# Selective-scan kernel: the carry between chunks added to column 0 of the scans' inputs, B rows and bias operands moved from ScalarE to TensorE, split of one product at 312 columns

## What is computed

```
layer 0:  v = group_norm(x, 32 groups);  u, z = split(v @ in_proj)          192 channels each
          u = silu(causal_conv_4(u) + conv_b)
          dt, B, C = split(u @ x_proj)                                      6 + 16 + 16
          delta = softplus(dt @ dt_proj + dt_bias);  A = -exp(A_log)
          h[t] = exp(delta[t] * A) * h[t-1] + delta[t] * B[t] * u[t]        192 channels x 16 states, 4096 steps
          y[t] = sum over states of h[t] * C[t]  + D * u[t]
          x = x + layer_norm((y * silu(z)) @ out_proj) * gamma + beta
layer 1:  t = t + linear attention(layer_norm(t));  t = t + feed-forward(layer_norm(t))   fp8 products, fp16 sums
```

## Time and profile before

| what | value |
|---|---|
| median of three runs | 2514.06 us |
| each run | 2515.68, 2513.10, 2514.06 us |
| span of the profiled execution, first to last instruction | 2508.8 us |
| what the median has beyond that span | 5.3 us |
| instructions in the profile | 35019 |
| mean granted TensorE clock | 0.987 |
| HBM read, written | 400.33 MB, 91.88 MB |

### The profile page before, as it was taken

One profiled execution on the slowest core, in us unless ns is written; L12 is line 12 of the kernel. 1 busy time (PEld: TensorE's weight loads), 2 busy tenths in 40 slices (PEclk: granted clock), 3 DMA queues, 4 the chain that ended last, 5 costly groups with the idle time before them and its releaser, 6 DMA issues.

```text
span 2508.8 us, 35019 instructions
## 1 busy us (share of the span) xinstructions
PE 2142.1 (85%) x10314; PEld 826.0 (33%) x10314; DVE 2454.5 (98%) x2391; ACT 2314.7 (92%) x3960; POOL 2414.8 (96%) x655
## 2 busy tenths in 40 slices
PE   6788888888888888888888888888888888888878
PEld 3334434323323323323333323323323333333323
DVE  7999999999999999999999999999999999999986
ACT  5777777999999999999999999999999999999977
POOL 4999999999999999999999999999999999999991
PEclk8999999999999999999999999999999999999979
DMA  6555555556656656566566566566566565566542
GB/s 243 189 185 172 195 185 184 202 198 207 209 202 205 207 201 212 201 205 206 204 206 214 194 208 212 195 210 208 198 210 211 197 207 201 192 206 203 186 142 75
DMA packets 171388, 494.54 MB, mean 197 GB/s; under 512 B 23072, under 2 KB 44704, under 8 KB 154240
## 3 DMA queue, kind: packets, MB, share of 16 engines
q1 hardware_dynamic: 171200, 492.30, 57.9%
HBM read 400.33 MB, written 91.88 MB: 196 GB/s over the span
## 4 chain that ended last, share of the span: by engine, by line
POOL 40%; issue 40%; DVE 15%; PE 3%; ACT 1%; DMA 0%; POOLq 0%; DVEq 0%; SPq 0%; ACTq 0%
POOL R L676 20%; DVE R L1277 11%; POOL D L649 9%; POOL R L672 7%; POOL du L642 3%; DVE D L1261 2%; POOL D L658 2%; PE G L1568 1%; PE Y L1568 0%; DVE q L1357 0%; DVE dl L1287 0%; DVE G L1302 0%; DVE h L1471 0%; DVE h L1478 0%; PE Y L1645 0%
## 5 line engine op out<-in xcount | busy, mean ns | idle before, releaser
L1277 DVE TENSOR_TENSOR_SCAN R<-DA,R,D 128x512 f32<-128x512 f32 x1344 | 1630.2, 1263 | 1.0 <-ACT DA L840 1.0
L840 ACT ACTIVATE DA<-ds,kept_w 128x512 f32<-128x512 f32 x1536 | 1054.8, 688 | 139.9 <-DVE R L1277 127.1
L676 POOL TENSOR_TENSOR R<-R,Cs 128x2048 f32<-128x2048 f32 x255 | 970.9, 3819 | 4.0 <-DVE R L1277 2.6
L649 POOL TENSOR_TENSOR D<-us,Bs 128x2048 f32<-128x2048 f32 x193 | 736.9, 3818 | 8.8 <-DMA us<-lo_d 8.8
L672 POOL TENSOR_TENSOR R<-R,Cs 128x4096 f32<-128x4096 f32 x64 | 476.5, 7446 | 0.1
L1261 DVE TENSOR_TENSOR D<-us,PB 128x2048 f32<-128x2048 f32 x191 | 356.8, 1868 | 6.3 <-DMA us<-lo_d 6.3
L1645 PE MATMUL Y<-R,kept_w 128*32 128x512 f32 x2048 | 266.1, 615 | 13.9 <-POOL R L672 12.8
L1602 PE MATMUL G<-un,wcv 96*128 96x512 f32 x512 | 251.6, 614 | 29.5 <-ACT h L907 29.5
L1277 DVE TENSOR_TENSOR_SCAN R<-DA,D 128x512 f32<-128x512 f32 x192 | 221.7, 1204 | 2.1 <-ACT DA L840 2.1
L1605 PE MATMUL G<-un,wcv 96*64 96x256 f32 x1024 | 138.5, 392 | 60.1 <-ACT xq L888 58.9
L1568 PE MATMUL G<-st,kept_w 128*64 128x256 f32 (+1 forms) x384 | 108.9, 485 | 53.5 <-ACT st L802 53.5
(11 more groups left out here) (240 smaller groups left out, 3437.5 us busy)
## 6 DMA issues: line engine op xcount, KB each, us to landing
Bs<-bc_d SPq DMA_DIRECT2D x128, 512.0 KB, 5.6
us<-lo_d SPq DMA_DIRECT2D x64, 1024.0 KB, 6.3
ds<-lo_d SPq DMA_DIRECT2D x64, 1024.0 KB, 8.4
Cs<-bc_d SPq DMA_DIRECT2D x128, 512.0 KB, 4.7
us<-hi_d SPq DMA_DIRECT2D x64, 512.0 KB, 6.8
ds<-hi_d SPq DMA_DIRECT2D x64, 512.0 KB, 5.5
lo_d<-dl SPq DMA_DIRECT2D x64, 256.0 KB, 2.0
lo_d<-du SPq DMA_DIRECT2D x64, 256.0 KB, 2.0
```

Of the source, the lines that this page charges most:

```text
L649: nc.gpsimd.tensor_tensor(shaped(D[:, s % NDBU, :, :], s), low(us, s) if s in LOWS else high(us), of_states(Bs, s), ALU.mult).then_inc(don ...
L676: nc.gpsimd.tensor_tensor(shaped(R[:, s, :, 0:T], s), shaped(R[:, s, :, 1:S], s), of_states(Cs, s), ALU.mult).then_inc(hc_done.sem, 1)
L840: nc.scalar.activation(DA[j % NDA][:, :], ds[:, i, :], ACT.Exp, scale=A[:, j:j + 1]).then_inc(exp_done.sem, 1)
L1277: nc.vector.tensor_tensor_scan(R[:, s, q, 1:S], DA[j % NDA][:, :], D[:, s % NDBU, q, :], before, ALU.mult, ALU.add).then_inc(scanned.sem, 1)
```

## The change

Three things. First, in a continuing chunk the scans of quads 1 to 5 no longer take their start value from R. In its place exp(delta[0] * A) * R's last column is added to column 0 of D: `first_product` (delta[0] * A, VectorE), `first_decay` (exp, ScalarE), `carries` (times R's last column, VectorE) for quads 1 to 3 together and for quads 4 and 5 together, and `take_carry` (add to column 0, VectorE) for each quad. Quad 0 keeps the pointer operand. The new calls stand in VectorE's iteration here: first_product (g, 0) behind scan (0, 0); carries (g, 0) behind scan (0, 1); take_carry 1 behind gate part 1; take_carry 2 behind scan (1, 0); first_product (g, 1) behind scan (2, 2); take_carry 3 behind scan (2, 3); carries (g, 1) behind scan (3, 1); take_carry 4 behind scan (3, 3); take_carry 5 behind scan (4, 2). ScalarE runs first_decay (g, 0) behind decay (0, 2) and first_decay (g, 1) behind decay (3, 0).

Second, `put_b` moves from ScalarE to TensorE: a matmul of st's 32 rows of B and C with a selection matrix writes B's rows spread over 128 rows into PB, without waiting for Bs. It stands first in TensorE's iteration (quad 1), behind out_proj (g - 1) (quad 3) and behind variance (g - 1, 1) (quad 0 of g + 1). st becomes double-buffered, with B and C in rows 0 to 31, dt in rows 32 on and a constant row of ones, so its eviction is a plain copy. The bias of the convolution becomes a 97th row of its first tap's matmul, and the epsilon under three logarithms a 97th row of the averaging matmul (rows of ones in un, sq and fsq, set by four memsets at the start).

Third, SPLIT[3] goes from 232 to 312 columns.

```diff
-SPLIT = {3: 232}
+SPLIT = {3: 312}
...
+        def goes_on(k):
+
+            return 0 <= k <= LAST and k % CH > 0
...
-        wcv = sb("wcv", [C, TAPS, 2 * LOW])
+        wcv = sb("wcv", [C + 1, TAPS, 2 * LOW])
...
-        un = sb("un", [C, HALO + T])
+        un = sb("un", [C + 1, HALO + T])
...
-        st = sb("st", [128, T])
+        st = sb("st", [128, 2, T])
...
+        first = sb("first", [128, QUADS, QUAD])
...
+        first_arg, first_exp = Continued("first_arg", 2), Continued("first_exp", 2)
+        first_carry, first_in = Continued("first_carry", 2), Continued("first_in", 5)
...
+        def first_of(v):
+
+            return first[:, 1:QUAD, :] if v == 0 else first[:, QUAD:QUADS, :]
...
             sp_eng.dma_start(cwb, I["conv_w"].partition_broadcast(C)).then_inc(cwb_in, 16)
+            sp_eng.dma_start(wcv[C:C + 1, 0, :], I["conv_b"]).then_inc(cb_in, 16)
...
-                    nc.scalar.activation(u[:, place(k) % 2, part(v)], src[v], ACT.Silu, bias=cb[:, v:v + 1])\
+                    nc.scalar.activation(u[:, place(k) % 2, part(v)], src[v], ACT.Silu)\
...
             def state_rows(k, src):
                 act.wait_ge(back_mm.sem, back_mm.at(k, 1))
-                act.wait_ge(back_mm.sem, back_mm.at(k - 1))
-                if there(k - 1):
-                    act.wait_ge(bc_out, count(k - 1, 16, 16))
-                nc.scalar.activation(st[:, :], src[:, :], ACT.Identity, bias=one_row).then_inc(st_done.sem, 1)
+                act.wait_ge(b_put.sem, b_put.at(k - 2))
+                if there(k - 2):
+                    act.wait_ge(bc_out, count(k - 2, 16, 16))
+                nc.scalar.copy(st[0:64, k % 2, :], src[0:64, :]).then_inc(st_done.sem, 1)
...
-            def put_b(k, s):
-                if k == 0 and s == 1:
-                    return
-                h, w = LOWS[s]
-                if s == 3 and place(k + 3) == 0 and later(k + 3):
-                    act.wait_ge(gn_act.sem, gn_act.at(k + 3, 4))
-                act.wait_ge(b_in[h], count(k, 16, 16))
-                act.wait_ge(dbu_d.sem, dbu_d.at(k, BY_DVE[s] - steps_to(k, s)))
-                n = SPLIT.get(s, T)
-                nc.scalar.copy(PB[:, 0:n], Bs[:, h, w, 0:n]).then_inc(b_put.sem, steps_to(k, s))
...
+            def first_decay(k, v):
+                act.wait_ge(first_arg.sem, first_arg.at(k, 1 + v))
+                nc.scalar.activation(first_of(v), first_of(v), ACT.Exp).then_inc(first_exp.sem, 1)
...
-                nc.scalar.activation(rs[:, :], src[0:C, :], ACT.Ln, bias=epsn[0:C, :]).then_inc(post_ln.sem, 1)
+                nc.scalar.activation(rs[:, :], src[0:C, :], ACT.Ln).then_inc(post_ln.sem, 1)
...
+            step(nc.vector.memset(sq[C:C + 1, :], 1.0))
+            step(nc.vector.memset(fsq[C:C + 1, :], 1.0))
+            step(nc.vector.memset(un[C:C + 1, :], 1.0))
+            step(nc.vector.memset(st[64:65, :, :], 1.0))
             credit(nc.vector, by_dve)
...
                     dve.wait_ge(summed.sem, summed.at(k - 1, s + 1))
-                before = 0.0 if place(k) == 0 else R[:, s, q, T:S]
+                    if s and goes_on(k):
+                        dve.wait_ge(first_in.sem, first_in.at(k, s))
+                before = R[:, s, q, T:S] if s == 0 and goes_on(k) else 0.0
...
+            def first_product(k, v):
+                dve.wait_ge(d_in[v], count(k, 16, 16))
+                if v == 0:
+                    a = A[:, QUAD:4 * QUAD].rearrange("p (s q) -> p s q", q=QUAD)
+                    d = ds[:, 0:QUAD, 0].unsqueeze(1).to_broadcast([128, 3, QUAD])
+                    o = first_of(v)
+                else:
+                    a = A[:, 4 * QUAD:BLOCKS].rearrange("p (w i) -> p w i", i=2)
+                    d = ds[:, QUAD:QUADS, 0].unsqueeze(1).to_broadcast([128, 4, 2])
+                    o = first_of(v).rearrange("p s (w i) -> p (s w) i", i=2)
+                nc.vector.tensor_tensor(o, a, d, ALU.mult).then_inc(first_arg.sem, 1)
+
+            def carries(k, v):
+                dve.wait_ge(first_exp.sem, first_exp.at(k, 1 + v))
+                dve.wait_ge(scanned.sem, scanned.at(k - 1, (4, 6)[v] * QUAD))
+                quads = slice(1, QUAD) if v == 0 else slice(QUAD, QUADS)
+                nc.vector.tensor_tensor(first_of(v), first_of(v), R[:, quads, :, T], ALU.mult).then_inc(first_carry.sem, 1)
+
+            def take_carry(k, s):
+                dve.wait_ge(first_carry.sem, first_carry.at(k, 1 if s in LOWS else 2))
+                if s in BY_DVE:
+                    dve.wait_ge(dbu_d.sem, dbu_d.at(k, BY_DVE[s]))
+                else:
+                    dve.wait_ge(dbu_p.sem, dbu_p.at(k, BY_POOL[s]))
+                at = D[:, s % NDBU, :, 0]
+                nc.vector.tensor_tensor(at, at, first[:, s, :], ALU.add).then_inc(first_in.sem, 1)
...
-                        last = mm(o[:, :], wcv[:, t, 0:LOW], un[:, t:t + T], start=(t == 0), stop=(t == TAPS - 1))
+                        last = mm(o[:, :], wcv[0:rows_of(t), t, 0:LOW], un[0:rows_of(t), t:t + T], start=(t == 0), stop=(t == TAPS - 1))
...
+            def put_b(k, s):
+                if k == 0 and s == 1:
+                    return
+                if s == 3 and place(k + 3) == 0 and later(k + 3):
+                    pe.wait_ge(gn_act.sem, gn_act.at(k + 3, 4))
+                pe.wait_ge(st_done.sem, st_done.at(k))
+                pe.wait_ge(dbu_d.sem, dbu_d.at(k, BY_DVE[s] - steps_to(k, s)))
+                n = SPLIT.get(s, T)
+                one(PB[:, 0:n], bsel[:, BY_DVE[s] - 1, :], st[0:2 * STATE, k % 2, 0:n]).then_inc(b_put.sem, steps_to(k, s))
...
-        "wx": wx, "one_row": consts["one_row"], "dtw": dtw, "D": cols_of(np.asarray(L0_conv_D)[chan], 2),
+        "wx": wx, "dtw": dtw, "D": cols_of(np.asarray(L0_conv_D)[chan], 2),
+        "bsel": np.stack([np.arange(32)[:, None] == 8 * h + 2 * (row[None, :] % NSUB) + w
+                          for h, w in ((0, 0), (0, 1), (1, 1))], 1),
```

More of the change, by code:

```diff
@@ L142, in at @@
                 return count(k, 1, LEAD + 1 - FIRST * CH)
+        class Continued(Progress):
+            def at(self, k, n=None):
+                return (k - batch(k) - 1) * self.per + (self.per if n is None else n)
         rows_of_R = sb("R", [128, QUADS, QUAD, S + 3])
@@ L171, in build @@
         soon = cols["kept"]["wx"][2]
-        wz, cb, dsk, wx, one_row, dtw = (W[n] for n in ("wz_in", "conv_b", "D", "wx", "one_row", "dtw"))
+        wz, dsk, wx, dtw = (W[n] for n in ("wz_in", "D", "wx", "dtw"))
         sumsel, A, wd, wo, avg = (W[n] for n in ("sumsel", "A_log", "skip", "woT", "avg"))
@@ L1031, in iteration @@
                     decay(g, 5, 0)
-                if there(g + 1):
-                    put_b(g + 1, 0)
                 if g == LAST:
@@ L1096, in beginning @@
                     act.wait_ge(front_mm.sem, front_mm.at(0, 1 + v))
-                    last = nc.scalar.activation(u[:, 0, part(v)], src[:, 0:T - H * v], ACT.Silu, bias=cb[:, v:v + 1])
+                    last = nc.scalar.activation(u[:, 0, part(v)], src[:, 0:T - H * v], ACT.Silu)
                     last.then_inc(silued.sem, 1)
@@ L1222, in _ @@
             for t in range(TAPS):
-                step(nc.vector.tensor_tensor(wcv[:, t, :], wxm, cwb[:, t, :], ALU.mult))
+                step(nc.vector.tensor_tensor(wcv[0:C, t, :], wxm, cwb[:, t, :], ALU.mult))
             dve.sem_inc(w_conv, 1)
@@ L1374, in iteration @@
                     scan(g, 0, 1)
+                if goes_on(g):
+                    carries(g, 0)
+                if there(g):
                     inputs(g, 1)
@@ L1383, in iteration @@
                     scan(g, 1, 0)
+                if goes_on(g):
+                    take_carry(g, 2)
+                if there(g):
                     scan(g, 1, 1)
@@ L1395, in iteration @@
                     scan(g, 2, 2)
+                if goes_on(g):
+                    first_product(g, 1)
+                if there(g):
                     inputs(g, 3)
                     scan(g, 2, 3)
+                if goes_on(g):
+                    take_carry(g, 3)
                 if there(g - 1):
@@ L1402, in iteration @@
                     scan(g, 3, 1)
+                if goes_on(g):
+                    carries(g, 1)
                 if place(g - 9) == 0 and early(g - 9):
@@ L1416, in iteration @@
                     scan(g, 4, 2)
+                if goes_on(g):
+                    take_carry(g, 5)
+                if there(g):
                     scan(g, 4, 3)
@@ L1601, in conv @@
                     if v == 0:
-                        last = mm(o[:, :], wcv[:, t, 0:LOW], un[:, t:t + T], start=(t == 0), stop=(t == TAPS - 1))
+                        last = mm(o[:, :], wcv[0:rows_of(t), t, 0:LOW], un[0:rows_of(t), t:t + T], start=(t == 0), stop=(t == TAPS - 1))
                         continue
                     for rows, cs in halves():
-                        last = mm(o[rows, 0:H], wcv[:, t, LOW:LOW + HIGH], un[:, t + cs.start:t + cs.stop],
```

(26 more changed lines are left out.)

59 lines of the change are left out of this document (36 added, 23 removed).

## The result

The changed kernel takes 3299.52 us (median of four runs, 3298.05 to 3301.48) against 2514.82 for the kernel before (four runs beside them): a ratio of 1.3131, 95% interval 1.3115 to 1.3146. That is 785 us slower, where the forecast was 10 us faster and its range ended at 2522. The profiled execution has a span of 3297.3 us.

The account below looks back on a forecast made before the run. VectorE and GpSimd were both full in the steady batch, GpSimd setting the pace in the early one. Seven steady batches -9.0, the early one -4.0, start +2.4: in all -10.6 from 2514.06, so 2504 us, range 2487 to 2522.

Parts of the forecast that it names:

- the price of the nine small VectorE operations: VectorE, each continuing chunk: two products, two carries and five adds were to cost +0.70 us in all.
- The high end: VectorE: upper estimate for the nine small operations, the whole 150 ns each, 1.35 us per continuing chunk.
- Scans: VectorE: 59 ns less in 20 of 24 scans with a constant start value, -1.18 us per continuing chunk.
- Split: Quad 3, every chunk: 320 elements move from GpSimd to VectorE, VectorE +0.33 us, GpSimd -0.57 us.
- Waits of the new operations nothing: VectorE: the new small operations' inputs from ScalarE and GpSimd would be ready in time, costed at nothing.
- ScalarE's relief: ScalarE loses some 2 us per chunk; both VectorE waits at the scaling by gamma go, -0.56 us per batch.
- TensorE's three matmuls nothing: TensorE: three more matmuls per chunk would fall in or before existing waits and cost nothing.
- The start +2.4: Opening: four memsets before VectorE's first statistics, 2.7 us, less 0.3 for three activations without pointer: +2.4 us.
- Rival 2: VectorE, between the scans: small operations at 150 ns each, whole 2540 us, slower than before; chance 0.17.

Follow-up runs that it names:

- the run with PSUM operands: Changed kernel with the second SBUF operand of all nine small operations replaced by PSUM columns, carry of quads 1 to 5 left out: 2503.00 us, repeated 2504.42 us.
- the moves alone: Changed kernel without its carry, split back at 232; B rows from TensorE, biases and epsilons in matmuls kept: 2519.05 us, ratio 1.0026 to the kernel before.

## Why the prediction was wrong

**The step that failed is the price of the nine small VectorE operations**: +0.70 us, between 0.52 and 1.35. They took 13.5. The fixed cost was taken from the 97x97 add, with the remark that it reads PSUM and the new ones don't; the 17 ns between a 256-element row of SBUF alone (L1223) and one with a PSUM operand were added for that. But L1223 stands in the opening, at a time when GpSimd has nothing to do, and could not show it. In the steady state VectorE's products, scans and adds before the change all have an operand in PSUM; B's rows are even copied to PB for VectorE alone, and GpSimd is busy 96% of the time. The one exception, the aggregation, doesn't wait. The high end, "the whole 150 ns each", was no bound at all.

The trace of the kernel before did hold the wait, in its last 30 us, where some operations on SBUF alone meet a GpSimd instruction. Two of one form there:

```profile
2495.86 0.34 DVE L1471 TENSOR_SCALAR h16b<-h16b,b1q 128x512 f16<-128x512 f16 x1
...
2497.25 1.25 DVE L1471 TENSOR_SCALAR h16b<-h16b,b1q 128x512 f16<-128x512 f16 x1
```

The second began while GpSimd was in an instruction that ran from 2496.54 to 2498.35, and ended 0.15 us behind it. Of 27 operations at L1471 the five that met GpSimd so lasted 0.92 to 1.30 us, and ended 147 to 153 ns behind it; the other 22 lasted 334 to 354 ns.

Without the wait the price was right: in the run with PSUM operands 128x4 adds last 135 ns and step by 51, the others by 57 to 77 (medians), 0.52 us for the nine and 0.59 with a few waits, and the steady batch takes 298.55 us where 299.16 were forecast. For operands in SBUF alone the changed kernel itself has the price: its 112 adds of 128x4 that did not wait stepped by 69 ns (median), where 70 was forecast.

- *Scans*: 59 ns forecast, 66 measured (1268 less 1202). Right.
- *Split*: the 128x1248 form 1.43 us forecast, 1.439 measured; GpSimd's rest 2174 to 1599 ns, -0.57. Right.
- *Waits of the new operations nothing*: no semaphore wait appears before them (idle 0.0 in each group). Right by the letter; the wait was inside the operation, where the profile counts it as busy.
- *ScalarE's relief*: both waits at the scaling by gamma go in the run with PSUM operands (0.4 us in all 63). Rows of rs 675 to 584 ns. Right, and in the changed kernel buried under 40.6 us of waits for the inverse deviation, at L1344.
- *TensorE's three matmuls nothing*: right in the steady state (a steady batch of the moves alone is 0.3 us shorter than before), not so in the last chunk, which became 2.2 us longer and was not costed.
- *The start +2.4*: 4.1 to 5.9 (the first scan in the changed kernel, the moves alone and the two runs with PSUM operands). The memsets were sized a little short (2.7 for 3.1) and 0.9 taken as hidden or given back; the fall of TensorE's clock in the longer wait was missed.
- *Rival 2*, dear operations, had the right place and sign with a chance of 0.17, and the wrong price: it ended at 150 ns each. What it lacked was a row that scales with GpSimd's instructions.

The Trainium skill's page Vector Engine (DVE) Microarchitecture Reference was cited for 75 ns plus 1.0417 a column, by estimate 79 to 88 ns for 4 to 12 columns. Without GpSimd in the way the steps here were somewhat shorter (51 to 77 in the run with PSUM operands). The section The DRAIN you can't avoid of the Trainium skill's page VectorE: DVE Perf Modes was said to disagree with the trace; it adds itself that a next operation that is not held starts earlier, and the overlap of 0.08 us in the earlier trace rows agrees with that. The rule that decided stands on the Trainium skill's page SBUF — State Buffer, section Who interferes with whom, as above, and was not looked for, because the question asked was what such an operation costs, not what else reads SBUF at that time.
